# Adjacency times layer-norm features in split fp32: how piece 0 is loaded, how chunks 6 and 7 of block 0 are multiplied, and where the unit steps stand

## The reference

```python
h = jnp.maximum(_layernorm(x, axis=-1), 0.0)      # eps 1e-05
x = x + (1.0 - 0.1) * (adj @ h) + 0.1 * h0
```

## Time and profile before

| | |
|---|---|
| median of 3 runs | 710.25 us (710.11 to 710.32) |
| the profiled execution's own time | 710.53 us |
| its span (first to last instruction) | 708.4 us |
| TensorE busy | 703.5 us, 99% of the span |
| VectorE, ScalarE, GpSimd busy | 634.5, 531.8, 26.8 us |
| transfers | 285.7 MB, 403 GB/s over the span |

### The profile page before, as it was taken

One profiled execution on the slowest core, in us unless ns is written; L12 is line 12 of the kernel. 1 busy time (PEld: TensorE's weight loads), 2 busy tenths in 40 slices (PEclk: granted clock), 3 DMA queues, 4 the chain that ended last, 5 costly groups with the idle time before them and its releaser, 6 DMA issues.

```text
span 708.4 us, 8165 instructions
## 1 busy us (share of the span) xinstructions
PE 703.5 (99%) x3086; PEld 577.8 (82%) x3086; DVE 634.5 (90%) x549; ACT 531.8 (75%) x463; POOL 26.8 (4%) x38
## 2 busy tenths in 40 slices
PE   9999999999999999999999999999999999999998
PEld 5878888888888888888888888888888888888886
DVE  4999999999999999999898888888988898889885
ACT  4899998788788787887776767676767676767673
POOL 1100000000000000000000000000000000000000
PEclk9999999999999999999999999999999999999999
DMA  9999999999999999999999999999999999999990
GB/s 364 419 418 418 419 419 416 419 418 416 421 415 418 420 417 419 417 417 422 417 402 415 407 412 384 382 399 412 413 421 405 423 420 422 421 421 422 414 412 20
DMA packets 46550, 285.74 MB, mean 403 GB/s; under 512 B 5168, under 2 KB 9520, under 8 KB 14000
## 3 DMA queue, kind: packets, MB, share of 16 engines
q1 hardware_dynamic: 46080, 283.99, 97.8%
q10 hardware_dynamic: 432, 1.25, 0.5%
HBM read 281.02 MB, written 4.19 MB: 403 GB/s over the span
## 4 chain that ended last, share of the span: by engine, by line
PE 94%; DMA 3%; DVE 1%; ACT 1%; SPq 0%; issue 0%; DVEq 0%
PE acc L457 16%; PE acc L453 16%; PE acc L452 16%; PE acc L436 15%; PE acc L441 15%; PE acc L430 15%; DMA raw<-wide_dram 3%; DVE a_lo L345 1%; ACT a_hi L301 0%; SPq L213 0%; SPq L196 0%; DVE stats L311 0%; ACT h_full L271 0%; DVE mean_var L321 0%; SPq L226 0%
## 5 line engine op out<-in xcount | busy, mean ns | idle before, releaser
L345 DVE TENSOR_TENSOR a_lo<-raw,a_hi 128x2048 fp32r<-128x2048 f32 (+1 forms) x292 | 582.4, 2010 | 58.1 <-ACT a_hi L301 57.1
L301 ACT ACTIVATE a_hi<-raw 128x2048 fp32r<-128x2048 f32 (+1 forms) x368 | 497.9, 1382 | 160.6 <-PE acc L457 100.1
L452 PE MATMUL acc<-a_hi,h_hi 128*128 128x512 f32 x512 | 199.2, 389 | 0.0
L453 PE MATMUL acc<-a_hi,h_lo 128*128 128x512 f32 x512 | 199.2, 389 | 0.0
L430 PE MATMUL acc<-a_hi,h_hi 128*128 128x512 f32 x504 | 167.9, 390 | 0.0
L436 PE MATMUL acc<-a_hi,h_lo 128*128 128x512 f32 x504 | 167.6, 389 | 0.1
L457 PE MATMUL acc<-a_lo,h_hi 128*128 128x512 f32 x512 | 136.8, 389 | 0.0
L441 PE MATMUL acc<-a_lo,h_hi 128*128 128x512 f32 x504 | 135.2, 389 | 0.1
L453 PEld LDWEIGHTS acc<-a_hi,h_lo 128*128 128x128 f32 x512 | 96.1, 188 | 20.0
L457 PEld LDWEIGHTS acc<-a_lo,h_hi 128*128 128x128 f32 x512 | 96.1, 188 | 19.9
L452 PEld LDWEIGHTS acc<-a_hi,h_hi 128*128 128x128 f32 x512 | 96.1, 188 | 19.9
(11 more groups left out here) (15 smaller groups left out, 30.5 us busy)
## 6 DMA issues: line engine op xcount, KB each, us to landing
raw<-tall_dram SPq DMA_DIRECT2D x128, 1024.0 KB, 8.3
raw<-wide_dram SPq DMA_DIRECT2D x126, 1024.0 KB, 11.1
res_sb<-res_dram SPq DMA_DIRECT2D x16, 512.0 KB, 9.9
x_sb<-x_dram SPq DMA_DIRECT2D x30, 128.0 KB, 11.1
out_dram<-finished SPq DMA_DIRECT2D x15, 256.0 KB, 8.5
raw<-early_dram ACTq DMA_DIRECT2D x2, 512.0 KB, 6.7
raw<-early_dram SPq DMA_DIRECT2D x2, 512.0 KB, 5.9
out_dram<-finished SPq DMA_DIRECT2D x2, 128.0 KB, 1.8
```

The costliest lines, as they stand in the source:

```text
L301: nc.scalar.activation(a_hi[:, q % SPLIT_SLOTS, cols], raw[:, q % RAW_SLOTS, cols], ACT.Copy).then_inc(hi_ready, 1)
L345: nc.vector.tensor_tensor(a_lo[:, q % SPLIT_SLOTS, cols], raw[:, q % RAW_SLOTS, cols], a_hi[:, q % SPLIT_SLOTS, cols].bitcast(fp32), ALU.s ...
L452: nc.tensor.matmul(bank, h_hi[:, k, :], a_hi[:, slot, cols], start=(k == 0), stop=False)
L453: nc.tensor.matmul(bank, h_lo[:, k, :], a_hi[:, slot, cols], start=False, stop=False)
```

## The change

Five things are edited.

1. **Piece 0.** Each of its halves of 1024 columns is now loaded as 64 rows by SyncE's queue and 64 rows by ScalarE's queue (`BY_ROWS`), and the semaphore of a half counts 32. x of blocks 1 to 3 stands on ScalarE's queue between the two halves of piece 0; half (1,1) follows.
2. **Piece 1.** Its chunks 4 and 5 stay plain fp32, chunks 6 and 7 are split as all later ones (`MIXED` is piece 1, `MIXED_FROM` is 2): two a_hi and two a_lo of 512 columns, and six fp32r matmuls in place of four native passes. They run as two L434, two L438, two L442 (lines of the changed kernel).
3. **a_lo** of pieces 2 to 9 (`FINE_LOW`) is made in four steps of 512 columns, not two of 1024.
4. **Unit steps.** For units due below piece 40 (`LATE` is 20, was 16) the statistics stand behind a_lo of piece d-6, the aggregate behind d-4 and the shift behind d-3. The load of x stays at d-5. For the two units due at pieces 32 and 36 the load moves from d-6 to d-5.
5. **Warm-up** of 20 matmuls, not 22.

The diff, without its blank lines:

```diff
@@ -23,7 +23,10 @@
 NATIVE_BLOCKS = 1
 NATIVE = NATIVE_BLOCKS * QUADS
+MIXED, MIXED_FROM = NATIVE - 1, QUAD // 2
 RAW_SLOTS, SPLIT_SLOTS = 6, 3
 EARLY, EARLY_LOW = 2, 40
@@ -33,7 +36,10 @@
 FINE = range(NATIVE, EARLY_LOW)
-BY_SCALAR = [(0, 1), (1, 1)]
+FINE_LOW = range(NATIVE, 10)
+BY_ROWS = [0]
+BY_SCALAR = [(1, 1)]
@@ -45,7 +51,8 @@
-LATE = 16
+LATE = 20
 LOAD_X_AT = {}
 STATS_AT, AGGREGATE_AT, SHIFT_AT = {}, {}, {}
 SCALE_AT, HIGH_H_AT = {}, {}
@@ -54,16 +61,13 @@
     _due = QUADS * _a
     if _a < LATE:
         LOAD_X_AT[_due - 5] = _u
-        STATS_AT[_due - 5] = [_a, _a + 1]
-        AGGREGATE_AT[_due - 5] = SHIFT_AT[_due - 4] = _u + 1
-        SCALE_AT[_due - 2] = _u
+        STATS_AT[_due - 6] = [_a, _a + 1]
+        AGGREGATE_AT[_due - 4] = SHIFT_AT[_due - 3] = _u + 1
     else:
         LOAD_X_AT[_due - 6] = _u
-        STATS_AT[_due - 6] = STATS_AT.get(_due - 6, []) + [_a]
-        STATS_AT[_due - 5] = [_a + 1]
+        STATS_AT[_due - 6], STATS_AT[_due - 5] = [_a], [_a + 1]
         AGGREGATE_AT[_due - 5] = SHIFT_AT[_due - 4] = _u + 1
-        SCALE_AT[_due - 2] = _u
-    HIGH_H_AT[_due - 1] = _u
+    SCALE_AT[_due - 2] = HIGH_H_AT[_due - 1] = _u
@@ -81,7 +85,7 @@
 for _n, (_, _at) in enumerate(FINISH):
     RES_LOAD_AT[44 + 10 * _n if _n < RES_RING else _at - 9] = _n
     RES_SUM_AT[45 + 10 * _n if _n < RES_RING else _at - 8] = _n
-WARM_UP = 22
+WARM_UP = 20
 def parts(q):
@@ -92,14 +96,16 @@
 def ends(q, halves):
-    if q in FINE and halves is PARTS:
+    if q == MIXED:
+        return list(range(MIXED_FROM + 1, QUAD + 1))
+    if q in FINE and halves is PARTS or q in FINE_LOW:
         return [1, 2, 3, 4]
     return [2, 4] if q in halves else [4]
 def steps(q, halves):
-    begin = 0
+    begin = MIXED_FROM if q == MIXED else 0
     for end in ends(q, halves):
         yield begin * PARTS.get(q, 1) // QUAD, slice(begin * SEG, end * SEG)
         begin = end
@@ -108,7 +114,7 @@
 def steps_through(q, halves, seg=QUAD - 1):
     own = next(i for i, end in enumerate(ends(q, halves)) if seg < end) + 1
-    return sum(len(ends(k, halves)) for k in range(NATIVE, q)) + own
+    return sum(len(ends(k, halves)) for k in range(MIXED, q)) + own
 def part_of(q, seg):
@@ -186,15 +192,12 @@
         def wait_landed(engine, q, i):
             if q in PARTS:
-                engine.wait_ge(part_landed[q % RAW_SLOTS][i], 16 * landed_turn(q))
+                engine.wait_ge(part_landed[q % RAW_SLOTS][i], (32 if q in BY_ROWS else 16) * landed_turn(q))
             else:
                 engine.wait_ge(raw_landed[q % RAW_SLOTS], 16 * landed_turn(q))
-        def load_part(engine, q, i, cols):
-            n = PARTS[q]
-            at = (i % (n // 2)) * (PIECE // n)
-            engine.dma_start(raw[:, q % RAW_SLOTS, cols],
-                             adj_early[q, i // (n // 2), :, at:at + PIECE // n]
+        def load_part(engine, q, i, cols, rows=slice(0, P)):
+            engine.dma_start(raw[rows, q % RAW_SLOTS, cols], adj_early[q, i, rows, :]
                              ).then_inc(part_landed[q % RAW_SLOTS][i], 16)
         def in_x(k):
@@ -219,7 +222,9 @@
                     sp.wait_ge(piece_used, q - RAW_SLOTS + 1)
                 if q in PARTS:
                     for i, cols in parts(q):
-                        if (q, i) not in BY_SCALAR:
+                        if q in BY_ROWS:
+                            load_part(sp, q, i, cols, slice(0, P // 2))
+                        elif (q, i) not in BY_SCALAR:
                             load_part(sp, q, i, cols)
                 else:
                     source = adj_wide[q - EARLY, :, :] if q < WIDE_PIECES else adj_tall[q - WIDE_PIECES, :, :]
@@ -286,17 +291,21 @@
                 scale_h(range(a, b)).then_inc(h_full_ready, 1)
-            act.dma_start(x_sb[:, 1:FIRST, :], x[:, 1:FIRST, :]).then_inc(x_landed[1], 16)
+            for q in BY_ROWS:
+                for i, cols in parts(q):
+                    load_part(act, q, i, cols, slice(P // 2, P))
+                    if i == 0:
+                        act.dma_start(x_sb[:, 1:FIRST, :], x[:, 1:FIRST, :]).then_inc(x_landed[1], 16)
             for q, i in BY_SCALAR:
                 load_part(act, q, i, dict(parts(q))[i])
             act.wait_ge(scale_ready, 1)
             scale_h(range(1, FIRST)).then_inc(h_full_ready, 1)
             act.wait_ge(first_h_ready, 1)
             high_h(0)
-            for q in range(NATIVE, PIECES):
+            for q in range(MIXED, PIECES):
                 for i, cols in steps(q, PARTS):
                     wait_landed(act, q, i)
-                    if cols.start == 0 and q >= NATIVE + SPLIT_SLOTS:
+                    if cols.start == 0 and q >= MIXED + SPLIT_SLOTS:
                         act.wait_ge(piece_used, q - SPLIT_SLOTS + 1)
                     nc.scalar.activation(a_hi[:, q % SPLIT_SLOTS, cols], raw[:, q % RAW_SLOTS, cols],
                                          ACT.Copy).then_inc(hi_ready, 1)
@@ -411,11 +420,28 @@
             pe.wait_ge(first_h_ready, 1)
             for q in range(NATIVE):
                 k, quad = q // QUADS, q % QUADS
-                for j in range(QUAD):
+                for j in range(MIXED_FROM if q == MIXED else QUAD):
                     wait_landed(pe, q, part_of(q, j))
                     last = nc.tensor.matmul(acc[:, quad * QUAD + j, :], h_full[:, k, :],
                                             raw[:, q, j * SEG:(j + 1) * SEG], start=(k == 0), stop=False)
-                last.then_inc(piece_used, 1)
+                if q < MIXED:
+                    last.then_inc(piece_used, 1)
+            k, quad, slot = MIXED // QUADS, MIXED % QUADS, MIXED % SPLIT_SLOTS
+            pe.wait_ge(h_hi_ready, unit_of(k) + 1)
+            for j in range(MIXED_FROM, QUAD):
+                pe.wait_ge(hi_ready, steps_through(MIXED, PARTS, j))
+                nc.tensor.matmul(acc[:, quad * QUAD + j, :], h_hi[:, k, :], a_hi[:, slot, j * SEG:(j + 1) * SEG],
+                                 start=(k == 0), stop=False)
+            pe.wait_ge(h_lo_ready, unit_of(k) + 1)
+            for j in range(MIXED_FROM, QUAD):
+                nc.tensor.matmul(acc[:, quad * QUAD + j, :], h_lo[:, k, :], a_hi[:, slot, j * SEG:(j + 1) * SEG],
+                                 start=False, stop=False)
+            for j in range(MIXED_FROM, QUAD):
+                pe.wait_ge(lo_ready, steps_through(MIXED, LOW_PARTS, j))
+                last = nc.tensor.matmul(acc[:, quad * QUAD + j, :], h_hi[:, k, :],
+                                        a_lo[:, slot, j * SEG:(j + 1) * SEG], start=False, stop=False)
+            last.then_inc(piece_used, 1)
             for q in range(NATIVE, WIDE_PIECES):
                 k, quad, slot = q // QUADS, q % QUADS, q % SPLIT_SLOTS
                 fresh = quad == 0 and (k == NATIVE_BLOCKS or k == UNITS[unit_of(k)][0])
```

## The result

The changed kernel takes **711.29 us** (median of 22 runs, 710.79 to 711.85), the kernel before 710.27 us in the same comparison (710.11 to 710.71, 22 runs). The profiled execution of the changed kernel took 711.34 us, with a span of 709.5 us; that is 1.1 us over the span of before.

The account below looks back on a forecast made before the run. PE, busy 703.5 of 708.4 us, bounds the kernel; only the first 44 us can gain. Terms 0.27 + 0.35 + 0.34 + 0.57 = 1.53 us, cut to 0.76 by piece 11's data, gave 709.5 us, range 708.8 to 710.1.

Parts of the forecast that it names:

- the part on the start: Loading of piece 0: first half there by about 5 us, first real weight load 0.27 us earlier, near 5.9 us.
- Nothing is lost: x of blocks 1 to 3 moves behind 256 KB, but DVE can't take it before 5.4 us: no cost.
- Chunks 6 and 7: Block 0: four native passes (1.71 us) become six split matmuls (1.36 us), 0.35 us less PE work.
- Unit steps and finer a_lo: Pieces 4 and 12: PE's holes behind late DVE work close, worth 0.34 and 0.57 us.
- The extra 0.15 us of DVE per piece: Pieces 2 to 9: four a_lo instructions instead of two cost DVE some 0.15 us a piece, costed at nothing.
- The cap: Piece 11: its data let PE come just 0.19 us earlier, so 0.77 of 0.96 us won are waited for again.
- A: Early transfers: all landings come 0.6 us or more earlier and the whole 1.53 us stays, 708.7 us; chance 0.10.
- B: Pieces 11 to 13: DVE is still late, only 0.19 us or less remains, 710.1 us; chance 0.14.
- C: First native passes: PE's clock rises late, passes take 0.86 instead of 0.43 us, up to 713.9 us; chance 0.04.

Follow-up runs that it names:

- e4: Changed kernel with each half of piece 0 shared by columns, 512 columns of all 128 rows on each of the two queues; 710.74 us.
- e1: Changed kernel with only the loading of piece 0 undone (halves of 128 rows on one queue each, x of blocks 1 to 3 first on ScalarE's queue); 709.37 us.
- e5: e1 with x of blocks 1 to 3 issued behind half (0,1) on ScalarE's queue; 709.67 us.
- e12: e1 with chunks 6 and 7 of block 0 back as native fp32 passes; 709.36 us.
- e13: e1 with the old tables of the unit steps and LATE at 16; 709.98 us.
- e14: e1 with a_lo in four steps up to piece 13 instead of 9; 709.14 us.
- e7: Changed kernel with x first and each half of piece 0 on one queue as two 64-row transfers, lower rows first on both queues; 714.51 us.
- e8: e7 with the upper 64 rows first on ScalarE's queue; 713.28 us.
- e3: Changed kernel with SyncE taking the even rows and ScalarE the odd rows of each half of piece 0; 711.04 us.

## Why the prediction was wrong

**The step that failed** is in the part on the start: the landing "stays, because the bytes ahead of it are the same", and with it the 0.41 MB/us taken from the earlier trace rows for the first transfers. The bytes were the same; the rate was not. The earlier trace rows only show transfers to all 128 rows, and I used them for 64 neighbouring rows. Instead of 0.41 it was 0.26 MB/us for five microseconds, and piece 2 landed 2.2 us later. By that landing 1.3 us come with the rows (13.65 against 12.31 us in e4) and 0.9 us with more and shorter transfers (12.31 against 11.43 us in e1); by the times the parts are 0.55 and 1.4 us, and how they divide is open. I bounded the cost of the edit by the bytes that go ahead of x, and not by the rate of a form of transfer that the trace didn't show. The rival that was missing is the one that happened: all landings later, slower than before.

*Start.* The first load was foretold at 5.9 us and came at 5.92, from 6.17, which is the 0.27 us of the sum. That was luck. But the releaser was wrong: half (0,0) landed at 5.82 us and not by about 5, and h_full was done at 5.25. The right time came from two errors against each other, as x of block 0 came 0.2 us sooner and not 0.3 us later. h_full was ready 0.22 us sooner than before; in e1, whose first transfers are those of before, it was 4.55 + 0.29 = 4.84 us, 0.63 us sooner, with a first load at 6.48 us. The first microseconds differ by some tenths between executions, so a term of 0.27 us there couldn't be read from one.

*x of blocks 1 to 3.* "Nothing is lost" holds for the time: it landed 2.3 us later and DVE took its statistics at 6.19 us, but e5 puts the price at 0.3 us.

*Chunks 6 and 7.* Foretold: 0.35 us of PE work, all of it waited for again. With whole halves the time agrees, e1 and e12 being equal to 0.01 us, but that it is waited for isn't shown: e13 had kept 0.31 us of it as far as piece 12. In the changed kernel it turned round in part: half (1,1) landed at 12.64 us and PE had to wait for a_hi until 13.43 us, 0.8 us behind the landing, where a native pass needs no a_hi.

*Unit steps and finer a_lo.* Piece 4's and piece 12's holes went as foretold; no wait on h_lo is left. e13 gives the spread 0.5 to 0.6 us, of 0.57 foretold. The extra 0.15 us of DVE per piece was hidden. With the old steps nothing is left inside the span: its median is 708.2 us in e13 and in the runs of before beside it.

*The cap.* Piece 11 as the tightest place was right for the changed kernel: its a_lo of 1024 columns is the only one that PE still waits for, with data 1.9 us and PE 1.6 us later than before. In e13 PE waits for it too, 0.16 us at 39.66 us. In e1 it doesn't, and e14 doesn't settle what finer steps there bring. Without the loading of piece 0, the forecast was 0.76 us less than before by 0.19 + 0.57; e1 measured 0.9 less, 709.37 against 709.5 us foretold. That agrees better than it should: inside the span, to which the terms belong, e1 has 0.5 us less by the medians, which is the 0.57 us of piece 12 with little or nothing of the 0.19, and 0.35 us come from outside.

*The rivals.* A falls: the data came later, not earlier. B falls: waits on DVE in pieces 12 and 13 are absent, and come back only with the old tables (e13). C wasn't seen in the change: by the starts in the trace its warm-ups stand 0.21 us apart up to 4.06 us and 0.11 us apart from 4.17 us, so the clock rose during them, and the native passes took 0.43 us from one weight load to the next (6.46 to 6.89 us), as in the earlier trace rows. (The windows view can't tell this: it has a granted clock of 1.00 from 3 us on for the kernel before too, whose warm-ups stay 0.21 us apart up to 5.1 us.) C did come in e7 and e8, where the first pass waited until 9.8 and 9.4 us. What of the slower side there was came by another way than C.

## What to carry to other kernels

Two queues that share one tile by the lower and the upper 64 rows move less than two that each bring all rows of a part: read the rate and the packet time, not the DMA share, which is full in both cases. A time for a transfer from the trace holds for that form only; where an edit changes the rows or the length of a transfer, bound it by half the rate too, and ask how many later transfers stand behind it: in the change a delay of 2.2 us at piece 2 was still 1.9 us at 43 us, though in e3 of 1.6 us only 0.6 were left. And before a saving of some tenths is credited to an edit, compare where the two profiles stand ahead of it: e14 had nearly all its lead before its edit began.
